# First cross attention of a twelve-sublayer decoder: heads in pairs, rounding on Pool, probabilities turned by transposing DMAs

## The reference, cut to what matters

```python
q = (x @ Wq + bq).reshape(1, B * N, H, hd)
kv = (cond @ Wkv + bkv).reshape(1, -1, 2, H, hd)
...
q = _fq_sym(q, axis=-1)      # scale by max|.|/127 of a head's 16 numbers, round, scale back
k = _fq_sym(k, axis=-1)
v = _fq_sym(v, axis=2)       # one scale for each column of v, over all 512 rows
attn = jnp.einsum('bhqd,bhkd->bhqk', q, k)
attn = jax.nn.softmax(attn.astype(jnp.float32), axis=-1)
attn = _fq_unsigned(attn, axis=-1)   # scale by max/255, round, scale back
...
x = _layernorm(x + (attn @ v) @ Wp + bp)
```

## Time and profile before

| | |
|---|---|
| time, median of 3 runs (lowest, highest) | 4110.76 us (4109.12, 4114.24) |
| profiled execution: its time, its span | 4110.44 us, 4108.4 us |
| busy share of the span: PE, DVE, ACT, POOL | 81%, 68%, 48%, 10% |
| L0X: preparation | 274.5 to 322.7 us of the span |
| L0X: from the first score to the end of the last exponential | 322.7 to 756.8 us |
| L0X: from there to the first instruction of the next sublayer | 756.8 to 776.8 us |
| mean granted clock of PE in the middle part | 0.63 |

### The profile page before, as it was taken

How to read it: one execution, slowest core, us unless ns; L and a number is a source line. 1 busy time by engine, 2 the same in 40 slices (tenths; PEclk the granted TensorE clock), 3 DMA queues, 4 the chain that set the end, 5 groups by cost and what they waited for, 6 DMA issues and landing times. The chain is left out here.

```text
span 4108.4 us, 59566 instructions
## 1 busy us (share of the span) xinstructions
PE 3335.9 (81%) x18333; PEld 2417.8 (59%) x18364; DVE 2798.4 (68%) x8822; ACT 1969.4 (48%) x5854; POOL 407.3 (10%) x495
## 2 busy tenths in 40 slices
PE   7967888697999999674569976559999999999565
PEld 5644545474777777463237764227777777777344
DVE  4667888537788887566964437866666666666597
ACT  4537888414555555123521112336666666666243
POOL 0000000001111110110111100001111111111100
PEclk9986666799999999876569988569999999999588
DMA  1000000100000000000000012000000000000000
GB/s 55 2 23 1 1 1 1 80 1 13 1 1 1 1 1 1 39 1 29 1 15 1 1 43 100 1 11 1 1 1 1 1 1 1 1 1 1 32 1 21
DMA packets 6585, 50.37 MB, mean 12 GB/s; under 512 B 256, under 2 KB 4480, under 8 KB 4608
## 3 DMA queue, kind: packets, MB, share of 16 engines
q1 hardware_dynamic: 6272, 46.57, 2.9%
HBM read 44.47 MB, written 2.10 MB: 11 GB/s over the span
## 5 line engine op out<-in xcount | busy, mean ns | idle before, releaser
L2162 DVE CUSTOM_DVE_ANT_0 L3A_masked<-ps,L3A_hidden,L3A_negrstd 128x128 f32<-128x128 f32 (+1 forms) x512 | 193.5, 415 | 324.7 <-PE ps L2053 235.0
L2111 ACT ACTIVATE L3A_probs<-L3A_masked,L3A_negmax 128x128 f32<-128x128 f32 (+1 forms) x512 | 228.6, 449 | 238.2 <-DVE L3A_negmax L2162 238.2
L331 PE MATMUL ps<-s_weights_b,s_XT 128*128 128x512 f32 (+1 forms) x648 | 302.5, 596 | 24.7 <-ACT L1A_qn L1969 9.1
L2081 PE MATMUL ps<-s_weights_b,L3A_OT 128*128 128x256 f32 x1024 | 265.7, 382 | 14.8 <-DVE s_R L2191 14.8
L331 PE MATMUL ps<-s_weights_b,s_Xc 128*128 128x512 f32 x512 | 244.2, 599 | 7.8 <-DVE L3A_rot L2026 3.3
L877 ACT ACTIVATE L0X_pf<-ps,L0X_negmax_scaled,L0X_qscale 128x512 f32<-128x512 f32 x256 | 209.4, 818 | 54.8 <-DVE L0X_negmax_scaled L923 53.5
L2034 POOL TENSOR_TENSOR L3A_rstd<-L3A_ve,s_mhalf 128x4 f32<-128x4 f32 x144 | 145.1, 1008 | 854.4 <-DVE L3A_ve L1994 854.4
L918 DVE TENSOR_REDUCE L0X_negmax<-ps 128x1 f32<-128x512 f32 x256 | 176.4, 689 | 55.4 <-PE ps L816 47.3
L2081 PEld LDWEIGHTS ps<-s_weights_b,L3A_OT 128*128 128x128 f32 x1024 | 175.7, 192 | 29.2 <-issue 15.9
L868 ACT ACTIVATE L0X_pT<-ps,L0X_less 128x512 bf16<-128x512 f16 x256 | 184.9, 723 | 9.7 <-PE ps L825 9.6
L331 PEld LDWEIGHTS ps<-s_weights_b,s_XT 128*128 128x128 f32 x648 | 124.4, 211 | 109.0 <-issue 68.1
(11 more groups left out here) (512 smaller groups left out, 9038.7 us busy)
## 6 DMA issues: line engine op xcount, KB each, us to landing
s_weights_b<-w_L3A SPq DMA_DIRECT2D x1, 9984.0 KB, 27.0
s_weights_b<-w_L1A SPq DMA_DIRECT2D x1, 7936.0 KB, 21.3
s_weights_a<-w_L2F SPq DMA_DIRECT2D x1, 4224.0 KB, 13.9
s_weights_b<-w_L1F SPq DMA_DIRECT2D x1, 3840.0 KB, 13.1
s_weights_b<-w_L3F SPq DMA_DIRECT2D x1, 3136.0 KB, 10.4
s_weights_a<-w_L2A SPq DMA_DIRECT2D x1, 2898.0 KB, 9.4
s_weights_a<-w_L0F SPq DMA_DIRECT2D x1, 2176.0 KB, 9.0
s_X<-x SPq DMA_DIRECT2D x1, 2048.0 KB, 8.5
```

Source lines behind the costliest of these rows:

```text
L331: last = pe.matmul(out, lhs(k), rhs(k), start=(k == 0), stop=(k == n - 1))
L2081: last = pe.matmul(c.bank(3)[:, j * DM:(j + 1) * DM], OT[:, u % 4, j * P:(j + 1) * P], w["wo"][:, h, :], start=(h == 0 and j == 0), stop=( ...
L2111: last = a.activation(pr[:, u % 4, cols], ms[:, u % 2, cols], ACT.Exp, bias=nmx[:, h, j:j + 1], scale=-1.0, accum_out=sm[:, h, j:j + 1])
L2162: last = eng.tensor_tensor_reduce(out=ms[:, u % 2, cols], in0=s[:, cols], in1=hidden[:, P - j * P:2 * P], scale=-1.0 if gated else nrs[:, ...
```

## The change

A unit of the loop is now a pair of neighbouring heads, with slots counted for each sequence (16 pairs), and all of the sublayer is one block. The main steps of a pair: PE makes two 128x512 scores into two banks (three pairs of banks); DVE takes both maxima with one reduction (128x1024 to 128x2) and scales each with the logarithm of 255 added, so that ACT's two exponentials give 255 times as much; Pool rounds the pair with one instruction (add and subtract 12582912) into bf16; SP issues one transposing DMA from `ph` to `pT`, both in SBUF; PE multiplies with the values, eight matmuls with 16 columns, six slots after the scores. The transposes of probabilities on PE, the copies out of PSUM on ACT and the rounding on DVE are gone. `ph` and `pT` have four buffers and four semaphores.

Side work is rearranged: Pool cuts the keys into parts and rounds and copies the queries (`pool_q`); the scale of the values goes into the weights `wp` once, where it was multiplied onto each output; the bias is added ahead of time on Pool (`Xb`); both halves of a sequence are handled by one instruction in several places; all side transposes and projections use one bank in turn (`pe_side`), each waiting until the one before has been read. The last sequence's end is done in the same loop.

```diff
@@ sublayer_l0_cross: the order of side work
+    PAIRS = TT * HEADS // 2
+    U = SEQS * PAIRS
+    SLOTS = range(U + PAIRS)
+    LN255 = float(np.log(255.0))
+    VALUE_LAG = 6
+    STEP_AT = {0: ("X", 1), 1: ("Q", 1), 6: ("T0", 1), 7: ("T1", 1), 9: ("oT", -1), 10: ("Y", -1)}
...
-        pf = S.sb("pf", [P, 3, KEYS])
-        ph = S.sb("ph", [P, 2, KEYS], F16)
-        pT = S.sb("pT", [P, 3, KEYS], BF16)
+        pf = S.sb("pf", [P, 3, 2, KEYS])
+        ph = S.sb("ph", [P, 4, 2, KEYS], BF16)
+        pT = S.sb("pT", [P, 4, 2, KEYS], BF16)
...
@@ queries: quantized on DVE, rounded and copied on Pool
+        def pool_q(p, i):
...
+            p(g.tensor_tensor(heads_of(flat(tmp[:]), 2 * HEADS), heads_of(flat(row[:]), 2 * HEADS), spread(inv[:], DH), ALU.mult))
+            p(g.tensor_scalar(tmp[:], tmp[:], MAGIC, MAGIC, ALU.add, ALU.subtract))
+            for j in range(TT):
+                for part in range(3):
+                    p(g.tensor_copy(parts(j)[:, part], heads_of(tmp[:, j, :])), q_parts if part == 2 else None, free=True)
...
@@ SP
+                for p in range(U):
+                    sp.wait_ge(steps_ready, p + 1)
+                    if p >= 4:
+                        sp.wait_ge(o_made, p - 3)
+                    sp.dma_start_transpose(out=pT[:, p % 4].rearrange("p x (t q) -> p (x t) q", q=P), in_=flat(ph[:, p % 4])).then_inc(
+                        turned[p % 4], 16)
...
@@ PE
+                def values(p):
+                    b, j, m = place(p)
+                    pe.wait_ge(turned[p % 4], 16 * (p // 4 + 1))
...
+                for s in SLOTS:
+                    if s < U:
+                        scores(s)
+                    if s in step_at:
+                        pe_side(pe, step_at[s])
+                    if 0 <= s - VALUE_LAG < U:
+                        values(s - VALUE_LAG)
...
-                def turn(u):
-                    pe.wait_ge(steps_ready, u + 1)
...
-                        last = pe.transpose(o[:, t * P:(t + 1) * P], ph[:, u % 2, t * P:(t + 1) * P], c.idh[:])
...
@@ ACT
-                def take(u):
-                    a.wait_ge(probs_turned, u + 1)
-                    if u >= 3:
-                        a.wait_ge(o_made, u - 2)
-                    a.activation(pT[:, u % 3, :], c.bank(6 + u % 2, F16)[:, 0:KEYS], ACT.Identity,
-                                 bias=less[:, 0:1]).then_inc(probs_ready, 1)
...
@@ DVE
-                    eng.tensor_scalar(ph[:, u % 2, :], pf[:, u % 3, :], 255.0, HALF_MAGIC, ALU.mult,
-                                      ALU.add).then_inc(steps_ready, 1)
...
+                    v(eng.tensor_reduce(nmx[:, p % 4, :], c.ps[:, 2 * (p % 3):2 * (p % 3) + 2, :], AX.X, ALU.max, negate=True))
+                    for x in range(2):
+                        at = j * HEADS + 2 * m + x
+                        v(eng.tensor_scalar(nms[:, p % 4, x:x + 1], nmx[:, p % 4, x:x + 1], qs[:, b % 2, at:at + 1], LN255,
+                                            ALU.mult, ALU.add), max_ready if x else None, free=True)
...
@@ Pool
+                    p(g.tensor_scalar(ph[:, u % 4], pf[:, u % 3], MAGIC, MAGIC, ALU.add, ALU.subtract), steps_ready, free=True)
```

More of the change, by code:

```diff
@@ L680, in rows_of @@
             return c.bank(bank, BF16).rearrange("p (c t) -> p c t", c=QCH)
[L683 to L706, removed]
+        def place(p):
+            b, r = p // PAIRS, p % PAIRS
+            return b, r // (PAIRS // TT), r % (PAIRS // TT)
@@ L734, in _ @@
+                pe.wait_ge(v_round, KC)
+                pe.wait_ge(k_rows, KT)
                 for t in range(KT):
                     for f in range(KC):
[L736 to L745, removed]
+                        last = pe.transpose(c.bank(2 + t // 2)[:, (t % 2) * DM + f * P:(t % 2) * DM + (f + 1) * P],
+                                            vT[:, f, t * P:(t + 1) * P], c.k["ident"])
+                    if t % 2:
+                        last.then_inc(v_turned, 1)
+                for x in steps[2:4]:
+                    pe_side(pe, x)
@@ L752, in _, with exps @@
-                S.act_xT(a)
-                for j in range(TT):
-                    act_take_q(a, 0, j)
+                def exps(p):
+                    b, j, m = place(p)
+                    a.wait_ge(max_ready, p + 1)
+                    if p >= 3:
+                        a.wait_ge(steps_ready, p - 2)
+                    for x in range(2):
+                        at = j * HEADS + 2 * m + x
+                        last = a.activation(pf[:, p % 3, x, :], c.bank(2 * (p % 3) + x), ACT.Exp, scale=qs[:, b % 2, at:at + 1],
+                                            bias=nms[:, p % 4, x:x + 1], accum_out=sm[:, b % 2, at:at + 1])
+                    last.then_inc(exp_ready, 1)
@@ new lines, in _ @@
+                a.wait_ge(S.loaded, 16)
+                for f in range(KC):
+                    a.wait_ge(v_made, f + 1)
+                    a.activation(vT[:, f, :], c.bank(4 + f), ACT.Identity, bias=w["bv"][:, f:f + 1]).then_inc(vT_ready, 1)
+                act_side(a, steps[0])
+                for f in range(KC):
+                    a.wait_ge(v_scaled, f + 1)
+                    a.activation(vT[:, f, :], vT[:, f, :], ACT.Identity, bias=c.magic[:, 0:1], scale=vsc[:, f, 2:3]).then_inc(v_round, 1)
@@ new lines, in _, with steps_of @@
+            @block.gpsimd
+            def _(g):
+                p = Counted(g, pool_step)
+                def steps_of(u):
+                    g.wait_ge(exp_ready, u + 1)
+                    if u >= 4:
+                        g.wait_ge(turned[u % 4], 16 * (u // 4))
+                    p(g.tensor_scalar(ph[:, u % 4], pf[:, u % 3], MAGIC, MAGIC, ALU.add, ALU.subtract), steps_ready, free=True)
+                p(g.memset(rq[:], 0.0))
+                for t in range(KT):
+                    x = kx[:, t % 2, :]
+                    g.wait_ge(k_rows, t + 1)
```

378 lines of the change are left out of this document (193 added, 185 removed).

## The result

The changed kernel takes 4167.3 us (median of 4 runs, 4166.5 to 4169.0) where the kernel before takes 4112.5 us (4 runs, 4109.1 to 4114.8): 1.013 times as long, with a 95% interval of 1.0117 to 1.0152. It is some 55 us slower. Forecast were 3937 us, faster by 173. The direction is wrong, though the time lies in the range: by luck, as its upper part was reserved for slow DMAs.

What follows compares the result with a forecast made beforehand. It saw PE, DVE and ACT, nearly full and waiting on each other, as the bound. Preparation 25, loop 285 and end 19 make 329 us against 502.3, so 4110.4 - 173 = 3937 us; 8-in-10 range 3905 to 4230.

Steps and rivals of the forecast that it cites:

- Pool, the step that failed: Loop, Pool's rounding of a pair, 1024 columns: taken as 1.3 us, between 1.04 and 2.1 from plain copies.
- Rival D: Loop: Pool is the bound, rounding at 2.1 us, 316 us for the loop, 3968 us in all; chance 0.04.
- Pool: 27 us, beside the others: Loop: Pool's rounding and side work for a sequence take 27 us, alongside three engines needing 29 to 30.
- The forecast's own sign against its mechanism: Loop: the mechanism is wrong if the pair's cadence is set by something other than PE, DVE and ACT.
- The value taken, 1.9 us and hidden: Loop, the transposing DMA of each pair: 1.9 us, under the pair's 2.2 us and so hidden.
- B: Loop: transposing DMAs are the bound at 2.2 to 3.4 us each, still faster; 4041 us at 3.04; chance 0.25.
- C: Loop: SP's one queue with transposing DMAs above 3.58 us makes it slower, 5209 us at 12.2; chance 0.26.
- the pieces: Transposing DMA: source rows of 256 bytes, 1024 pieces; at a packet each the DMA takes 3.04 us.
- The waiting: Loop: a factor of 1.2 on engines needing 29 to 30 us, giving 35.6 us a sequence, 285 in all.
- slower: Whole kernel over 0.2% slower, through transposing DMAs above 3.58 us in SP's queue; chance 0.26.
- The preparation: Before the loop: key cutting moves to Pool beside DVE, 25 us to the first score, 23 saved.
- The end of the stage: After the loop: loses a barrier and two DVE passes, gains Pool's rounding and a landing, 19 us against 20.0.

Runs made afterwards that it cites:

- e4: Changed kernel, but ACT writes the exponentials as uint8 and Pool only casts them to bf16, without the two operations: 3989.2 us, 0.970 of the kernel before.
- e7: e4 with two transposing DMAs of 128x512 to a pair, one for each head, in place of one of 128x1024: 4013.3 us, 0.976 of the kernel before.
- e6: e5 with the two projections of a sequence cut into halves in neighbouring slots, second halves one slot later: 3952.1 us, 0.961 of the kernel before.
- e5: e4 with the side steps set further apart, five places in the slot table changed: 3957.0 us, 0.962 of the kernel before.
- e2: Changed kernel without rounding of the probabilities; the exponential writes bf16 straight into the buffer the DMA reads: 3982.7 us, 0.969 of the kernel before.

## Why the prediction was wrong

**Pool, the step that failed: "Below it is bounded by a plain copy of as many, 1.04 us, above by two of them, 2.1, as it does two operations."** It measured 3.63. The upper end was an argument, not a row: it supposed that one instruction with two operations costs at most what two copies do. No instruction of this form on Pool stood in the trace of before, so nothing measured closed the range from above. The slower time followed from that. Rival D named the mechanism, the place and the signs to look for, and had a chance of 0.04 and a time of 3968 us because it took 2.1 us as the worst. With 3.60 from start to start and side work of 6.9 as measured (it had 5.9), its formula gives 16 x 3.60 + 6.9 = 64.5 us a sequence, 516 for the loop, 560 with the ends, and 4110.4 + 58 = 4168 us, where 4166.5 were profiled. "Pool: 27 us, beside the others" should have been 64, twice what the other three need. The forecast's own sign against its mechanism, a cadence set by something other than these three, came true.

The Trainium skill's "GPSIMD Engine Reference", section Engine selection, says of Pool that with one input it runs at roughly line rate. The cast of e4 agrees (1.04 us for 1024 columns), the scalar form with one input does not (2.77 and 3.63), and the measurement decides.

**DMA.** The value taken, 1.9 us and hidden, was near enough: 1.23 us of the queue, 3.1 to the landing. Rivals B and C, with half of the chance, had no part in it, and e7 shows the room: twice the issues, 2.5 us, and it is felt. B was right about the pieces: there are (135,424 - 256) / 128 = 1,056 packets under 512 bytes to a DMA (last section). It was wrong about the pace: e6 has a pair every 2.30 us, below B's 3.04, with landings of 3.2, so that DMAs overlap. From the DMA engines' share of 0.64 there, one is an estimated 0.64 x 2.30 = 1.5 us of all 16. That the time came out slower, with a chance of 0.26 given to "slower", is luck: those 0.26 stood for slow DMAs alone. The Trainium skill's "VectorE: DVE Perf Modes", section The three transpose paths, gives 1309 ns for a 128x128 block through the DMA, from which the prediction estimated 10.5 us for eight. A landing after 3.1 us with eight blocks refutes that estimate. The Trainium skill's "DMA: Bandwidth & Descriptors", section Latency and other measured facts, gives 261 GB/s for transposing DMAs, from which it estimated 1.0 us. That is too little for a kernel to plan with, since the queue takes 1.27 us even for half the data.

**The waiting, a term mis-sized.** A factor of 1.2 on some 30 us was taken. With DVE's beat as measured (1.50 us where 1.42 was forecast) and the forecast's 6.3 of side work, a sequence is 24.0 + 6.3 = 30.3 us of DVE's work. In e4, with Pool out of the way, it took 16 x 2.58 = 41.3: a factor of 1.36. e5 and e6 bring it to 37.4 and 36.7, factors of 1.23 and 1.21. So what went beyond the forecast's factor was the order of the side steps, each waiting for a copy that ACT has behind its exponentials. The forecast had counted side work by its length and not by what each step waits for. What e6 still loses was not taken apart further.

**Other sizes.** Two scores of a pair take 0.61 us and the reduction 1.22, as forecast. The preparation was 29.4 us against 25. The rows of its end:

```profile
293.27 0.18 DVE L763 TENSOR_SCALAR L0X_inv<-L0X_inv 128x32 f32<-128x32 f32 x1
...
294.90 1.06 POOL L776 TENSOR_TENSOR L0X_tmp<-L0X_row,L0X_inv 128x512 f32<-128x512 f32 x1 [2.09 <-PE ps L699]
296.05 1.93 POOL L777 TENSOR_SCALAR L0X_tmp<-L0X_tmp 128x512 f32<-128x512 f32 x1
298.04 2.12 POOL L780 CAST L0X_rq<-L0X_tmp 128x256 bf16<-128x256 f32 x6
```

DVE is done at 293.5 where 291.8 was forecast. Pool starts 1.4 us later, as PE must first have read `rq`. Its rounding takes 1.93 us where 0.6 was put, the same error as in the loop. Together they make the 4 us. The end of the stage was forecast at 19 us. Counted as in the earlier trace rows, from the last exponential, it is 27.2: with Pool the bound its last roundings, 3.6 us each, trail behind ACT.

## What to carry to other kernels

An idle engine is not a free one: before work moves to it, take the duration of that very form of instruction on that engine from a trace, or measure it; a copy of the same size says nothing about it. If no row has it, leave the range open at the top and ask at what cost the engine becomes the bound (here Pool makes the stage longer than before from (502.3 - 44) / 8 = 57.3 us a sequence on, with its 5.9 of side work (57.3 - 5.9) / 16 = 3.2 us for a rounding, where 2.1 had been taken as the worst); give that case a chance of its own. And when three engines pass work round, count for each side step what it waits for, not only how long it is: moving five of the six, with what hangs on them, was worth 32 us.

## What the runs showed of the hardware

- Pool's scalar form on 128x1024 from f32 to bf16 took 3.63 us with two operations and 2.77 with one, DVE's 0.73 with two; a Pool cast from uint8 to bf16 took 1.04.
- ACT writing uint8 costs the same as f32, 785 and 773 ns for 512 columns, so that cutting to whole steps came for nothing there.
- A transposing DMA from SBUF to SBUF took 1.23 us of SP's queue for 128x1024 and 1.27 for 128x512, and landed after 3.1 and 2.5 us. Its packets are small ones: 135,424 of the 141,736 packets of the run are under 512 bytes, where it was 256 of 6,585 before. The DMA engines' share over the loop was 0.64 at the fastest cadence (e6).
- Some instructions of DVE take longer beside Pool's long ones. The clearest is the addition of a constant to 128x2 numbers, first in the loop of the changed kernel, then in that of e2, where Pool rounds nothing; below them the same addition and the two roundings around it on the timeline:

```profile
L259 DVE TENSOR_SCALAR s_ve<-s_mv x7: 1118/1121/1124, 408.9 to 790.7; 128x2 f32<-128x2 f32 x7
L259 DVE TENSOR_SCALAR s_ve<-s_mv x7: 168/168/169, 374.2 to 621.8; 128x2 f32<-128x2 f32 x7
...
405.36 7.22 POOL L948 TENSOR_SCALAR L0X_ph<-L0X_pf 128x1024 bf16<-128x1024 f32 x2
408.90 1.12 DVE L259 TENSOR_SCALAR s_ve<-s_mv 128x2 f32<-128x2 f32 x1
```

1.12 us and 0.17. All seven in the changed kernel start 0.06 us before a rounding does and end 1.1 us into it, 2.6 before its end. The norm's scaling of 128x256 numbers (L266) took 0.41 to 1.13 us, and 0.40 to 0.41 in e2. It does not hold for all: a scaling of 128x32 numbers on DVE (L763), at 313.75 in the middle of the rounding from 311.20 to 314.83, takes its 0.18 us. The reductions from PSUM are untouched, 1220 and 1217 ns. The Trainium skill's "SBUF — State Buffer", section Who interferes with whom, says that DVE and GpSimd share a pair of ports, that one of them holds it for its whole instruction, and that the scalar form can take it and a reduction doesn't. The reductions agree; that the addition ends long before the rounding does not fit a hold for the whole instruction. What lengthens it no run shows. DVE had time to spare in that kernel, busy for 28.7 of 60 us.
